# The second row of x1 is loaded at the end of product 4, into the place of A22 and S1, and split at the change of layers

## What is computed

```python
def _L0_cond_ref(x, language_ids, W, Wr, A, B):
    base = jnp.einsum('btd,od->bto', x, W)
    logits = jnp.einsum('btd,ed->bte', x, Wr) + bias[:, None, :]
    topw, topi = jax.lax.top_k(logits, TOP_K)
    ...
    h = jnp.einsum('btd,erd->bter', x, A)
    lora_out = jnp.einsum('bter,bte,eor->bto', h, gates, B)
    return base + SCALING * lora_out

def _L1_cond_ref(x, adapter_ids, weight):
    w = weight[adapter_ids]
    return jnp.einsum('bsi,boi->bso', x, w)
...
x = x + _L0_cond_ref(x, itok_B_0_7, ...)
x = x + _L1_cond_ref(x, itok_B_0_15, L1_cond_weight)
```

## Time and profile before

| what | value |
|---|---|
| median of three runs | 413.41 us (413.06 to 414.33) |
| the profiled execution | 414.52 us, of it 412.5 us span |
| TensorE busy | 398.8 us, 97% of the span |
| VectorE busy | 316.5 us, 77% |
| ScalarE busy | 171.4 us, 42% |
| GpSimd busy | 53.7 us, 13% |
| granted clock of TensorE, mean | 0.992 of full speed |
| layer 1 | first matmul 226.04 us, last one 408.38 us from the span's start |

### The profile page before, as it was taken

The page is one execution under the profiler, slowest core; times in us unless marked ns, Lnnn a source line. Parts: engine busy times, 40 slices in busy tenths (PEclk is TensorE's granted clock), DMA queues, the critical chain, the costliest instruction groups (busy, mean ns, idle before and its releaser), DMA issues.

```text
span 412.5 us, 5971 instructions
## 1 busy us (share of the span) xinstructions
PE 398.8 (97%) x1920; PEld 336.1 (81%) x1920; DVE 316.5 (77%) x412; ACT 171.4 (42%) x231; POOL 53.7 (13%) x80
## 2 busy tenths in 40 slices
PE   8999989899999999999999994999999999999996
PEld 8989868688889888888888883888888888888884
DVE  2999999998357468239887567999999899999600
ACT  2342342664220132344272235565565555565411
POOL 1010100000000100000210022314225222324000
PEclk9999999999999999999999997999999999999999
DMA  8977520133376300008592999999999999997211
GB/s 189 222 210 200 147 60 0 52 103 102 94 223 201 95 0 2 1 2 229 131 327 91 354 230 310 248 294 284 302 276 293 284 279 281 287 285 191 76 52 51
DMA packets 78577, 72.79 MB, mean 176 GB/s; under 512 B 7090, under 2 KB 77266, under 8 KB 77522
## 3 DMA queue, kind: packets, MB, share of 16 engines
q1 hardware_dynamic: 51584, 47.21, 46.6%
q10 hardware_dynamic: 26962, 25.21, 19.5%
HBM read 55.61 MB, written 16.78 MB: 175 GB/s over the span
## 4 chain that ended last, share of the span: by engine, by line
PE 72%; DVE 13%; DMA 4%; issue 4%; SPq 4%; ACT 1%; POOL 1%; ACTq 0%; DVEq 0%
PE banks L1166 13%; PE banks L1168 13%; PE banks L1167 12%; PE banks L1069 9%; PE banks L1071 9%; PE banks L1070 9%; SPq L377 4%; PE banks L1062 4%; DMA raw<-in_L_cond_weight_dram 2%; DVE weights L468 2%; DVE turned_w_f L456 2%; PE banks L1080 1%; PE banks L1082 1%; PE banks L1081 1%; DMA raw<-in_x_dram 1%
## 5 line engine op out<-in xcount | busy, mean ns | idle before, releaser
L1069 PE MATMUL banks<-ring,weights 128*128 128x512 f32 x192 | 75.2, 391 | 2.7 <-DVE weights L468 1.4
L424 POOL TENSOR_TENSOR raw<-raw,ident 128x128 f32<-128x128 f32 x50 | 36.2, 725 | 263.5 <-DMA raw<-in_L_cond_weight_dram 224.2
L1166 PE MATMUL banks<-weights,tokens 128*128 128x512 f32 x176 | 68.5, 389 | 0.0
L1167 PE MATMUL banks<-weights,tokens 128*128 128x512 f32 x176 | 68.5, 389 | 0.0
L1168 PE MATMUL banks<-weights,tokens 128*128 128x512 f32 x176 | 68.5, 389 | 0.0
L935 ACT ACTIVATE weights<-weights_f 128x1024 fp32r<-128x1024 f32 x44 | 46.6, 1060 | 48.4 <-DVE weights_f L612 47.1
L612 DVE STREAM_TRANSPOSE weights_f<-raw 128x1024 f32<-128x1024 f32 x42 | 51.7, 1233 | 6.6 <-POOL raw L424 6.1
L618 DVE TENSOR_TENSOR weights<-weights_f,weights 128x1024 fp32r<-128x1024 f32 x44 | 52.3, 1191 | 0.0
L1071 PE MATMUL banks<-ring,turned_w 128*128 128x512 f32 x128 | 49.8, 389 | 0.0
L1070 PE MATMUL banks<-tokens,weights 128*128 128x512 f32 x128 | 49.8, 389 | 0.0
L1069 PEld LDWEIGHTS banks<-ring,weights 128*128 128x128 f32 x192 | 36.0, 188 | 10.9 <-DVE weights L468 1.8
(11 more groups left out here) (113 smaller groups left out, 619.4 us busy)
## 6 DMA issues: line engine op xcount, KB each, us to landing
raw<-in_L_cond_weight_dram SPq DMA_DIRECT2D x168, 128.0 KB, 6.9
ring_f<-in_L_cond_weight_dram SPq DMA_DIRECT2D x88, 128.0 KB, 6.9
raw<-in_x_dram SPq DMA_DIRECT2D x64, 128.0 KB, 3.4
x_kept<-stage ACTq DMA_DIRECT2D x32, 256.0 KB, 4.1
out_dram<-sums ACTq DMA_DIRECT2D x32, 256.0 KB, 6.8
raw<-in_L_cond_W_dram SPq DMA_DIRECT2D x32, 128.0 KB, 3.1
sums<-x_kept ACTq DMA_DIRECT2D x3, 1024.0 KB, 8.7
stage<-x_kept ACTq DMA_DIRECT2D x3, 1024.0 KB, 8.9
```

Source lines behind the costliest of these rows:

```text
L424: nc.gpsimd.tensor_tensor(spot, spot, ident[:].rearrange("p (q j) -> p q j", q=Q), ALU.add)\
L1069: nc.tensor.matmul(ps, u_hi, x_hi, start=first and k == 0, stop=False, skip_group_check=True)
L1166: nc.tensor.matmul(l1_bank(o), x_hi, w_hi, start=m == 0, stop=False)
L1167: nc.tensor.matmul(l1_bank(o), x_hi, w_lo, start=False, stop=False)
```

## The change

The load of row 1 of x1 is issued right behind that of row 0, at the end of product 4 of the second span, and lands in slots 4 and 5 of `turned_w` (`turned_w_f` is the same memory seen as plain float32), where low parts of A22 and S1 were. Its high part is made in one go behind `load_x1` and `x1_high` of row 0, ahead of the stores of quarter "12"; the wait for the end of product 3 moves from the load to it, since it writes into `tokens`, which product 3 reads. Its low part is made ahead of `turn_w1(8)`, so before group 2's low part is written over the place where it landed. Rows 2 to 7 keep their order.

```diff
--- before.py
+++ after.py
@@ -352,9 +352,12 @@
             return of[:, at:at + 2]
 
 
+
         def x1_landed(row):
-            if row < 2:
+            if row == 0:
                 return x1_place(row, 1, tokens_f)
+            if row == 1:
+                return turned_wf[:, HM:HM + 2]
             return stage[:] if row % 2 == 0 else sums2[:].rearrange("p (s a) f -> p s (a f)", s=2)
 
         def x1_part(row, low):
@@ -773,15 +776,14 @@
             x1_low(0)
             for r in range(HM):
                 add_up(1, "12", r)
+            x1_low(1)
             turn_w1(8)
             turn_w1(9)
             low_w1(8)
             for n in range(10, NW1):
                 turn_w1(n)
                 low_w1(n - 1)
-                if n == M + 5:
-                    x1_low(1)
-                elif n > M + 5 and n % M == 2:
+                if n > M + 2 and n % M == 2:
                     x1_low(n // M)
             low_w1(NW1 - 1)
 
@@ -904,10 +906,8 @@
                 nc.scalar.activation(kept_slot(e), main_bank(s, r), ACT.Copy).then_inc(c21_copied, 1)
 
             def load_x1(row):
-                if row == 0:
+                if row < 2:
                     act.wait_ge(steps, product_end(1, 4))
-                elif row == 1:
-                    act.wait_ge(steps, product_end(1, 3))
                 elif row == 3:
                     act.wait_ge(summed_up, added_at(1, "12", HM - 1) + 1)
                 elif row >= 4:
@@ -919,7 +919,9 @@
 
             def x1_high(row):
                 act.wait_ge(x1_loaded[row % 2], (row // 2 + 1) * 16)
-                if row >= 2:
+                if row == 1:
+                    act.wait_ge(steps, product_end(1, 3))
+                elif row >= 2:
                     act.wait_ge(l1_ready, (row - 1) * 2 * TT)
                 for j in range(2):
                     nc.scalar.activation(x1_place(row, 0)[:, j], x1_landed(row)[:, j],
@@ -996,6 +998,7 @@
                 highs("x", s, 3)
                 if s:
                     load_x1(0)
+                    load_x1(1)
                     high_w1(4)
                     high_w1(5)
                 for r in range(HM):
@@ -1021,7 +1024,7 @@
                 copy_u2(1, r)
             gT_high(1)
             span(1)
-            load_x1(1)
+            x1_high(1)
             keep_all(1, "12")
             high_w1(8)
             load_x1(3)
@@ -1034,8 +1037,6 @@
                 row, last = o // (2 * TT), o % (2 * TT)
                 if o == 0:
                     load_x1(2)
-                elif o == 1:
-                    x1_high(1)
                 elif last == 0 and row + 3 < NB:
                     load_x1(row + 3)
                 elif last == 2 * TT - 1 and row + 2 < NB:
```

## The result

The changed kernel takes 408.48 us, the median of six executions (406.56 to 411.38); the kernel before 413.38 us, the median of its six. The ratio is 0.988, with a 95% interval of 0.984 to 0.992. So it is faster, by 4.9 us where 8.4 were forecast, and it lies above the range. Two further measurements gave 407.70 and 406.99 us (ratios 0.986 and 0.983). All 17 executions lie between 406.51 and 411.38; their median is 407.48, at the upper edge of the range, and the last of the three medians lies inside it.

A forecast was written before the change was run, and what follows sets the result against it. TensorE, busy 398.8 of 412.5 us, was taken as the bound, so only its idle or slow-clock time could be won: -5.55 - 2.90 + 0 + 0 = -8.45 us, from 413.41 to 405.0 us, range 404.0 to 407.5.

The forecast's parts named there:

- The gap and its cause: Layer 1, TensorE's 96th to 97th matmul: waits for row 1's low part, not its load; 5.55 us won.
- The clock: Layer 1, behind the gap: granted clock stays 1.00 instead of 0.51 for 6.07 us; 2.90 us won.
- The early load: Row 1's load, issued at 209.92 us right behind row 0's, makes neither row 0 nor the stores late: cost 0.
- The stream of weights: Layer 1, groups 4 to 15: weights come 4.6 us earlier, over the 3.0 us needed; no wait, cost 0.
- Two things: VectorE not stopping between pieces 13 and 14 (at least 1.2 us); 1.05 MB less queued (up to 3.4 us).
- The lower bound: Layer 1's weight stream gains only 1.2 us, from VectorE alone; waits then add up to 1.8 us.
- the 3.0 us to be covered: Layer 1, group 12: complete at 359.64 us, wanted at 356.6 without the gap, so 3.0 us short.
- the weights become the bound: Layer 1: weights come too late, waits at even groups; 1.8 us, 406.8 us (409.7 if clock falls); chance 0.21.
- From the profiled execution to the median: Whole kernel: runs' median taken as 1.1 us under the profiled execution, so 413.41 - 8.45 = 404.96 us.

The follow-up runs named there:

- the split alone: The kernel before with only the making of row 1's high and low parts moved, its load unmoved; 410.79 us, ratio 0.991.

## Why the prediction was right and wrong

- **The gap and its cause** were right. Row 1's high part now starts at 223.80 (223.5 was expected), its low part ends at 229.4 (229.5), and the 5.55 us are gone. That the load was never the late part is shown by the split alone, which removes the gap with the load where it was.
- **The clock** was right in the profiled executions: 1.00 throughout layer 1, with waits of up to 1.68 us. The Trainium skill (TensorE: Matmul & The Clock Gate, HAM oscillation) tells of idle gaps behind which the next matmuls run at half rate. The trace agrees: 5.38 us of idle time brought 0.51, and waits of 0.76 to 1.68 us left it at 1.00. In executions without a trace the mean clock reads 0.994 to 1.000; where it was lower isn't shown.
- **The early load** was right to cost nothing where it stands. The first load landed 5.3 us after its issue, as before, and the second after 8.7 us, at 219.4, 4.4 us before it was used. Layer 1 started at 226.26 instead of 226.04.
- **The stream of weights** is the step that failed: "Two things bring it forward ... I take 4.6, which is over 3.0: no wait, cost 0." At group 4 the stream came 0.2, 1.6 and 3.2 us earlier in the three profiled executions, not 4.6. The prediction priced the removed load at up to 3.4 us for pieces 9 to 17, as if the queues drained the rest at once. Pieces 9 and 10 kept 1.4 to 2.4 us of it; then piece 11 travelled beside row 3's load and arrived between 0.9 us later and 1.3 us earlier than before, and piece 17 came 0.3 us later than before in the first of the three. That the removed load is worth something is probable, as the split alone is 3.1 us slower. The lower bound, 1.2 us from VectorE alone, was no bound at all: the split alone is that case, and its last matmul is 5.0 us late, not 1.8. Relief on VectorE brings nothing forward where the pieces arrive late. And the 3.0 us to be covered came from one execution. In the first of the changed kernel group 8 was complete at 318.06, 2.7 us later than the 315.4 of before; pieces 25 and 33 were late there, behind loads of rows. In the other two it was complete at 313.34 and 312.43.
- **The rival** "the weights become the bound" is what came, with the signature named for it: waits at even groups. Its price of 1.8 us is near the 2.2 us between the first median and the fastest version without waits (408.48 - 406.3), which is in part luck: the other two medians leave 1.4 and 0.7 us, and the price was worked out from the bound that didn't hold. Its chance of 0.21 was too low.
- **From the profiled execution to the median** a second step failed: "The runs' median is 1.1 us under the profiled execution: 413.41 - 8.45 = 404.96." The version with pieces 9 and 10 early, without a wait in layer 1 in either profile, takes 406.3 and 406.6, which is near what the profiled execution alone gives: 414.52 - 8.45 = 406.1. That the kernel before varies through the very gap that the change removes would explain it, since its executions lie between 412.7 and 415.3 us and the ten of that version within 0.8 us; only one of its executions was profiled, so this is argued and not shown. The floor was set 1.3 to 1.6 us too low by it, and with 1.8 us of waits on the right floor the forecast would have been 407.9 to 408.4.

## What to carry to other kernels

When the wait that bounds a kernel is taken away, everything behind it is asked for earlier by as much; compare each later arrival with its new hour, and read its spread from more than one execution. A supply that has kept pace only because the consumer stood still once has no lead, and freeing the engine that handles it gives none while its transfers are late: use stretches in which nothing moves to start it earlier. A gain read in one profiled execution is best taken off that execution's own time, not off the median.

## What the runs showed of the hardware

- Alone in the queues, the weights move at 234 GB/s with a DMA share of 1.15, so a piece of 0.52 MB takes 2.2 us, about as long as VectorE's work on it (2.3 us); while loads of rows and stores run alone, from 212 to 214 us, the traffic is 385 GB/s at a share of 0.96.
- A load of 1.05 MB beside this stream mostly holds up one piece, whichever of them it is, rather than each a little: GpSimd waits 5 to 8 us for that one, and 1 to 2 us for most others. Now and then it is two pieces by some 4 us each (pieces 16 and 17 in the changed kernel's first profiled execution, 4.03 and 3.80).
- Of two such loads issued 0.54 us apart on the same queue, the first was delayed little: it landed after 5.3 us in the changed kernel's first profile and after 5.3 to 7.0 us in all eleven profiles with both loads, against 5.3 to 6.0 us in the three where it was alone. The second took 8.5 to 9.2 us.
